# First stage of a bidirectional-WKV, attention and expert kernel: backward scan without the own key, minima read from PSUM and placed later, small vectors loaded first

## What is computed

```python
ek = exp(min(k, 30));  ekv = ek * v
nf[t] = nf[t-1] * decay + ekv[t];   df[t] = df[t-1] * decay + ek[t]      # forward in time
nb[t] = nb[t+1] * decay + ekv[t];   db[t] = db[t+1] * decay + ek[t]      # backward in time
euk = exp(min(u + k, 30))
num = nf + nb - ekv + euk * v
den = df + db - ek + euk
c = sigmoid(r) * (num / max(den, 1e-8)) * (0.8 + 0.2 * tf)
```

## Time and profile before

| what | value |
|---|---|
| median of three runs | 2295.05 us |
| the profiled execution's own time | 2294.41 us |
| its span | 2292.7 us |
| busy in the span: PE, DVE, ACT, POOL | 93%, 59%, 51%, 63% |
| end of the first stage (first instruction of the next) | 113.7 us |
| first query matmul, last one | 64.0 us, about 111 us |

### The profile page before, as it was taken

How to read it: one execution, slowest core, us unless ns; L and a number is a source line. 1 busy time by engine, 2 the same in 40 slices (tenths; PEclk the granted TensorE clock), 3 DMA queues, 4 the chain that set the end, 5 groups by cost and what they waited for, 6 DMA issues and landing times. The chain is left out here.

```text
span 2292.7 us, 39955 instructions
## 1 busy us (share of the span) xinstructions
PE 2143.2 (93%) x11247; PEld 1862.4 (81%) x11247; DVE 1349.4 (59%) x2499; ACT 1160.3 (51%) x2491; POOL 1439.5 (63%) x961
## 2 busy tenths in 40 slices
PE   2899999999999999999899989999999999999996
PEld 1678888888878878777777778989999999998874
DVE  8868888778856676766765433333333333333386
ACT  4477777787767767767652123333333333333310
POOL 7887777787755656666672311466677777653365
PEclk9999999999999999999998999999999999999998
DMA  5444444533365536665335543556667676664566
GB/s 129 140 124 133 129 134 161 169 118 100 121 232 163 161 116 211 216 197 185 115 128 202 203 143 118 159 168 185 192 189 210 185 210 187 200 194 134 171 199 205
DMA packets 367657, 380.29 MB, mean 166 GB/s; under 512 B 51556, under 2 KB 283560, under 8 KB 362728
## 3 DMA queue, kind: packets, MB, share of 16 engines
q1 hardware_dynamic: 255608, 252.20, 36.0%
q10 hardware_dynamic: 96496, 75.28, 10.6%
q0 software_dynamic: 15360, 50.34, 6.7%
HBM read 264.21 MB, written 120.59 MB: 168 GB/s over the span
## 5 line engine op out<-in xcount | busy, mean ns | idle before, releaser
L2066 POOL TENSOR_SCALAR we_high<-we_raw 128x1408 fp32r<-128x1408 f32 (+1 forms) x94 | 132.2, 1406 | 312.3 <-PE up_e L668 231.6
L2068 POOL TENSOR_TENSOR we_low<-we_raw,we_high 128x1408 fp32r<-128x1408 f32 (+1 forms) x94 | 312.2, 3321 | 7.8
L2281 DVE TENSOR_TENSOR hidden_e<-silu_e,up_e 128x352 f32<-128x352 f32 x127 | 66.2, 522 | 250.1 <-ACT silu_e L2220 248.3
L2264 DVE TENSOR_TENSOR hT_low<-hT_ps,hT_high 128x256 fp32r<-128x256 f32 x127 | 53.9, 425 | 253.1 <-ACT hT_high L2206 249.5
L2220 ACT ACTIVATE silu_e<-gate_e 128x352 f32<-128x352 f32 x127 | 59.1, 465 | 283.7 <-PE up_e L668 278.6
L668 PE MATMUL gate_e<-we_high,xT_high 128*128 x508 | 176.2, 347 | 11.5 <-DVE xT_low L2271 6.4
L2225 ACT ACTIVATE rows_out<-down_e 128x512 f32<-128x512 f32 x127 | 76.0, 599 | 198.6 <-PE down_e L668 194.2
L668 PE MATMUL gate_e<-we_high,xT_low 128*128 x508 | 164.5, 324 | 0.0
L668 PE MATMUL up_e<-we_high,xT_high 128*128 x508 | 164.3, 323 | 0.0
L668 PE MATMUL gate_e<-we_low,xT_high 128*128 x508 | 164.1, 323 | 0.0
L668 PE MATMUL up_e<-we_high,xT_low 128*128 x508 | 164.0, 323 | 0.0
(11 more groups left out here) (401 smaller groups left out, 7168.7 us busy)
## 6 DMA issues: line engine op xcount, KB each, us to landing
slots_out<-rows_out ACTq DMA_DIRECT2D x127, 256.0 KB
rows_early<-slots_in ACTq DMA_DIRECT2D x500, 64.0 KB
we_raw<-L_ffn_w_gate SPq DMA_DIRECT2D x32, 704.0 KB, 4.9
we_raw<-L_ffn_w_up SPq DMA_DIRECT2D x32, 704.0 KB, 5.2
w_ring<-L_attn_Wq SPq DMA_DIRECT2D x64, 256.0 KB
q_T<-q_out SPq DMA_DIRECT2D x64, 256.0 KB, 2.3
w_ring<-L_attn_Wk SPq DMA_DIRECT2D x64, 256.0 KB
w_ring<-L_attn_Wv SPq DMA_DIRECT2D x64, 256.0 KB
```

The lines of the kernel that those rows point to most:

```text
L2066: nc.gpsimd.tensor_scalar(wh[:, p, at:to], raw[:, at:to], 1.0, 1.0, ALU.mult, ALU.mult).then_inc(w_hi, 1)
L2068: nc.gpsimd.tensor_tensor(wl[:, p, at:to], raw[:, at:to], wh[:, p, at:to].bitcast(F32), ALU.subtract).then_inc(w_split, 1)
L2281: nc.vector.tensor_tensor(hb[:], sg[:], psu[:], ALU.mult).then_inc(h_done, 1)
```

## The change

1. The backward scans run over the keys from the second on and write 511 elements: b[t] = (b[t+1] + src[t+1]) * decay, the own key left out; the last element is set to zero once, at the start. So the difference dl = eu - ek falls away, and the sums take `eu` in its place. `eu` gets a ring of four tiles.
2. The two minima read the PSUM bank `psk` and no longer the copy `kt`; the next transposes into that bank wait for the minima too.
3. The orders of TensorE, ScalarE, VectorE and GpSimd change.
4. SyncE issues the eight small vectors first; the time embedding goes to ScalarE's queue, second after the first keys, and keys 2 and 3 from there to SyncE's queue. The time embedding and keys 1 have semaphores of their own.
5. ScalarE copies keys 0 (`t0`) before it waits for the small vectors.

```diff
+EU_RING = 4
 FIRST_PE = (
-    "k0 v0 k1 x0 k2 x1 k3 k4 x2 k5 k6 x3 x4 k7 x5 Q0 Q1 Q2 Q3 Q4 x6 Q5 Q6 Q7 Q8 Q9 Q10 x7 Q11 Q12 Q13 Q14 Q15 "
+    "k0 v0 k1 x0 k2 x1 k3 x2 k4 x3 k5 x4 Q0 k6 x5 Q1 Q2 k7 Q3 Q4 x6 Q5 Q6 Q7 Q8 Q9 Q10 x7 Q11 Q12 Q13 Q14 Q15 "
 FIRST_ACT = (
-    "t0 t1 E0 E1 h0 F0 t2 h1 E2 h2 h3 t3 c0 F1 h4 E3 t4 h5 c1 h6 F2 h7 F3 E4 F4 t5 h8 E5 c2 h9 c3 e0 t6 h10 e1 t7 "
+    "t0 t1 E0 E1 h0 F0 t2 h1 E2 h2 h3 t3 c0 F1 h4 E3 t4 h5 c1 h6 F2 h7 F3 h8 c2 t5 h9 F4 c3 E4 E5 h10 e0 t6 e1 t7 "
     "h11 E6 e2 F5 e3 e4 F6 e5 c4 E7 e6 e7 h12 e8 h13 e9 c5 h14 e10 e11 h15 F7 e12 c6 e13 e14 c7 e15 "
 FIRST_DVE = (
-    "m0 m1 s0 s1 m2 f0 m3 l0 s2 f1 m4 l1 s3 f2 m5 f3 l2 l3 s4 m6 s5 f4 m7 s6 f5 l4 s7 f6 l5 f7 l6 l7 "
+    "m0 m1 s0 s1 m2 f0 m3 l0 s2 f1 l1 s3 f2 l2 f3 l3 m4 m5 s4 s5 f4 m6 l4 s6 m7 f5 l5 s7 f6 l6 f7 l7 "
 FIRST_POOL = (
-    "o0 p0 o1 p1 a0 a1 o2 q0 p2 q1 q2 o3 q3 a2 p3 q4 q5 a3 o4 q6 p4 q7 q8 o5 q9 p5 q10 a4 q11 o6 a5 p6 o7 p7 q12 "
+    "o0 p0 o1 p1 a0 a1 o2 q0 p2 q1 q2 o3 q3 a2 p3 q4 q5 a3 q6 q7 q8 o4 p4 q9 o5 p5 q10 a4 q11 o6 a5 p6 o7 p7 q12 "
     "q13 a6 q14 a7 q15 "
...
-            sp.dma_start(te[:], cond.partition_broadcast(P)).then_inc(v_in, 16)
             for at, v, n in vec:
                 sp.dma_start(rows[at:at + n, :], v.rearrange("(r p) -> r p", p=P)).then_inc(v_in, 16)
+            for n in range(2, KC):
+                sp.dma_start(kin[:, n, :, :], column(fs, n)).then_inc(k_in[1], 16)
...
-            def other_products(n):
+            def other_product(n):
                 p = n % 2
-                tt(dl[:, p, :], eu[:, p, :], ek[:, p, :], ALU.subtract).then_inc(products_done, 1)
-                pool.wait_ge(products_done, 3 * n + 2)
-                tt(dk[:, p, :], dl[:, p, :], kt[:, p, :], ALU.mult).then_inc(products_done, 1)
+                tt(dk[:, p, :], eu[:, n % EU_RING, :], kt[:, p, :], ALU.mult).then_inc(products_done, 1)
...
                 if n >= 2:
                     pe.wait_ge(kt_done, n - 1)
+                    pe.wait_ge(min_done, n - 1)
...
-            for n in range(KC):
-                act.dma_start(kin[:, n, :, :], column(fs, n)).then_inc(k_in[1 if 0 < n < KC else 0], 16)
+            act.dma_start(kin[:, 0, :, :], column(fs, 0)).then_inc(k_in[0], 16)
+            act.dma_start(te[:], cond.partition_broadcast(P)).then_inc(te_in, 16)
+            act.dma_start(kin[:, 1, :, :], column(fs, 1)).then_inc(k1_in, 16)
...
                 if n >= 2:
-                    act.wait_ge(products_done, 3 * (n - 1))
+                    act.wait_ge(products_done, 2 * (n - 1))
                 nc.scalar.activation(kt[:, n % 2, :], psk[n % 2][:], ACT.Copy).then_inc(kt_done, 1)
...
+            order = list(FIRST_ACT)
+            turns(order[:1], t=keys)
             act.wait_ge(x_T, 1)
             nc.scalar.activation(cols[:], psv, ACT.Copy).then_inc(cols_done, 1)
...
             nc.vector.memset(one[:], 1.0)
-            dve.wait_ge(v_in, 16 * (len(vec) + 1))
+            for last_of in (nb, db):
+                nc.vector.memset(last_of[:, :, S - 1:S], 0.0)
+            dve.wait_ge(te_in, 16)
...
                 if n >= 2:
-                    dve.wait_ge(products_done, 3 * (n - 1))
+                    dve.wait_ge(products_done, 2 * n - 3)
                     dve.wait_ge(scan_done, n - 1)
-                nc.vector.tensor_scalar(ek[:, p, :], kt[:, p, :], 30.0, None, ALU.min)
-                nc.vector.tensor_scalar(eu[:, p, :], kt[:, p, :], cols[:, V_U1 + i:V_U1 + i + 1], 30.0, ALU.add,
+                nc.vector.tensor_scalar(ek[:, p, :], psk[p][:], 30.0, None, ALU.min)
+                if n >= EU_RING:
+                    dve.wait_ge(sums_done, 2 * (n - EU_RING + 1))
+                nc.vector.tensor_scalar(eu[:, n % EU_RING, :], psk[p][:], cols[:, V_U1 + i:V_U1 + i + 1], 30.0, ALU.add,
                                         ALU.min).then_inc(min_done, 1)
...
                 col = dec[:, n:n + 1].broadcast_to([P, S])
+                after = dec[:, n:n + 1].broadcast_to([P, S - 1])
                 for f, b, src in ((nf, nb, ekv), (df, db, ek)):
                     nc.vector.tensor_tensor_scan(f[:, p, :], col, src[:, p, :], 0.0, ALU.mult, ALU.add)
-                    last = nc.vector.tensor_tensor_scan(b[:, p, ::-1], col, src[:, p, ::-1], 0.0, ALU.mult, ALU.add)
+                    last = nc.vector.tensor_tensor_scan(b[:, p, 0:S - 1][:, ::-1], src[:, p, 1:S][:, ::-1], after, 0.0,
+                                                        ALU.add, ALU.mult)
```

More of the change, by code:

```diff
@@ L105, in first_gates @@
         small = sb("small", [P, 64])
-        kt, ek, eu, ekv, dl, dk = (two(f"g0_{n}") for n in ("kt", "ek", "eu", "ekv", "dl", "dk"))
+        kt, ek, ekv, dk = (two(f"g0_{n}") for n in ("kt", "ek", "ekv", "dk"))
+        eu = sb("g0_eu", [P, EU_RING, S])
         nf, nb, df, db = (two(f"g0_{n}") for n in ("nf", "nb", "df", "db"))
@@ L117, in first_gates @@
         psv, dec = vec_ps[:, 0:V_N], vec_ps[:, P:P + N]
-        v_in = sem("v_in")
+        v_in, te_in, k1_in = sem("v_in"), sem("time_in"), sem("k_in_second")
         k_in, x_in = [sem("k_in_first"), sem("k_in_rest")], [sem("x_in0"), sem("x_in1")]
@@ L212, in sums @@
                 pool.wait_ge(scan_done, n + 1)
-                tt(nb[:, p, :], nf[:, p, :], nb[:, p, :], ALU.add)
-                tt(db[:, p, :], df[:, p, :], db[:, p, :], ALU.add).then_inc(sums_done, 1)
+                tt(nf[:, p, :], nf[:, p, :], nb[:, p, :], ALU.add)
+                tt(df[:, p, :], df[:, p, :], db[:, p, :], ALU.add).then_inc(sums_done, 1)
                 pool.wait_ge(sums_done, 2 * n + 1)
[L216 to L220, removed]
+                pool.wait_ge(products_done, 2 * n + 2)
+                tt(nf[:, p, :], nf[:, p, :], dk[:, p, :], ALU.add)
+                tt(df[:, p, :], df[:, p, :], eu[:, n % EU_RING, :], ALU.add).then_inc(sums_done, 1)
+            turns(FIRST_POOL, o=first_product, p=other_product, q=low, a=sums)
         @block.tensor
@@ L226, in keys @@
             def keys(n):
-                pe.wait_ge(k_in[0 if n == 0 else 1], 16 if n == 0 else 16 * (KC - 1))
+                if n == 0:
+                    pe.wait_ge(k_in[0], 16)
+                elif n == 1:
+                    pe.wait_ge(k1_in, 16)
+                else:
+                    pe.wait_ge(k_in[1], 16 * (KC - 2))
                 if n >= KC:
@@ L252, in vectors @@
             def vectors(n):
-                pe.wait_ge(v_in, 16 * (len(vec) + 1))
+                pe.wait_ge(v_in, 16 * len(vec))
                 nc.tensor.transpose(psv, rows[:], ident[0:V_N, 0:V_N]).then_inc(x_T, 1)
@@ L276, in exponentials @@
                 nc.scalar.activation(ek[:, p, :], ek[:, p, :], ACT.Exp)
-                nc.scalar.activation(eu[:, p, :], eu[:, p, :], ACT.Exp).then_inc(exp_done, 1)
+                nc.scalar.activation(eu[:, n % EU_RING, :], eu[:, n % EU_RING, :], ACT.Exp).then_inc(exp_done, 1)
             def factor(n):
@@ L308, in _ @@
             nc.scalar.activation(small[:, 8:16], small[:, 0:8], ACT.Exp, scale=-1.0).then_inc(s_chain, 1)
-            order = list(FIRST_ACT)
-            turns(order[:1], t=keys)
             act.wait_ge(t_chain, 1)
@@ L338, in scans @@
                 p = n % 2
-                dve.wait_ge(products_done, 3 * n + 1)
+                dve.wait_ge(products_done, 2 * n + 1)
                 if n >= 2:
```

## The result

The changed kernel takes 2310.25 us (median of 11, 2304.8 to 2319.18) beside 2299.19 us of the kernel before (11 runs in all, 2294.31 to 2309.56): ratio 1.0047, 95% interval 1.0031 to 1.0063, so 7 to 14.5 us slower. The forecast was 13.6 us slower (2308.0). That 2308.0 and 2310.25 lie so close is in part luck: the forecast started from 2294.41, and the median of the kernel before over 11 runs is 2299.19.

What follows compares the result with a forecast made beforehand. VectorE's and GpSimd's recurrence was taken to bound the first stage until Q0, then TensorE's queries beside that recurrence. The gain to Q0, two stalls, slow restarts and smaller terms summed to +13.6 on 2294.41, giving 2308.0 us; range 2297 to 2316.

Steps and rivals of the forecast that it cites:

- Rival (c): TensorE after Q0: the queries stay unbroken if unit 6's exponentials are over by about 73 us, time 2290; chance 13%.
- (d): VectorE's swapped backward scan costs as attention's median one: +1.06 on sixteen scans, +17 us, 2325; chance 5%.
- (e): VectorE's minima: PSUM does not help them beside GpSimd, m stays at 2, +4 us, 2312; chance 4%.
- The slow restarts: TensorE after each of its two waits: Q4 and Q8 run slowly, 5.38 us against 2.72 warm; +2.7 us each.
- first pause: TensorE before Q4: it waits for the eviction of Q2 to empty a bank, from 73.5 to 81.0 us; +7.5.
- second pause: TensorE before Q8: it waits for the eviction of Q6, from 95.2 to 99.2 us; +4.0.
- gain to Q0: Start of the first query on TensorE: 57.9 us in place of 64.0; -6.1.
- k6, x5, k7 among the queries: TensorE after Q0: these three turns now run among the queries; +1.9 us or so.
- slow Q4: TensorE after its first wait: this query costs 5.4 us; +2.7.
- slow Q8: TensorE after its second wait: this query is slow again and ends at 104.5 us; +2.7.
- the tail: End of the first stage, from Q9's gated chunk through the last fractions; +0.9 us.
- Rival (b): The same stalls on TensorE but milder, without slow restarts or with two more gained at the start: +8, 2302.5; chance 10%.

Runs made afterwards that it cites:

- one order taken back: The changed kernel with m6, m7 and l4 to l7 back in their old places on VectorE; ratio to the kernel before 0.9967.
- old orders: The changed kernel's operations and early loads with all four orders of the kernel before; ratio to the kernel before 0.9955, in a second set of runs 0.9953.
- the evictions first: The changed kernel with ScalarE's order alone altered, evictions moved ahead of the exponentials of units 6 and 7; ratio to the kernel before 0.9991.

## Why the prediction was right

Right, by its own steps:
- The two stalls, their places, their releasers and about their sizes: 7.5 and 4.0 us forecast, 9.0 and 4.1 measured. Rival (c), unbroken queries, fell: Q3 ended at 69.5 and E6 began at 76.62. So did (d) (scan 1.19) and (e) (minima 0.68 and 0.74). PSUM made m 1.3 us, as taken from L334.
- The slow restarts. The granted clock is 0.50 from 74 us on, inside the first pause, and Q4, begun at 78.49, was evicted from 83.41: 4.9 us in place of 2.7. In the second pause the clock reads 1.00 (92 to 96) and then 0.55 (96 to 98); Q8 took 4.6 us.
- The cause was shown, not only argued: the orders alone reproduce both pauses, one order taken back removes both, and l4 to l6 taken back remove the second.

Off in size: the sum says 13.6, the stage end moved by 9.7. Its terms, with a query's length from its first matmul to the start of its eviction:

| term | forecast | measured |
|---|---|---|
| gain to Q0 | -6.1 | -8.6 |
| Q0 shorter than before (4.5 for 5.4) | not in the sum | -0.8 |
| k6, x5, k7 among the queries | +1.9 | +1.15 |
| first pause | +7.5 | +9.0 |
| slow Q4 | +2.7 | +2.2 |
| second pause | +4.0 | +4.1 |
| slow Q8 | +2.7 | +1.9 |
| what is left, the tail | +0.9 | +0.8 |

- The start was the largest miss. I took the first minima at 9.0 and the first scan at 13.2; they came at 7.0 and 11.1. The small vectors were there by 6.3, three us sooner than 9.3 before, and I had allowed for two at most, so that my bounds (8.5 to 9.95) did not hold the value. That is 2.1 of the 3.9 us.
- Slow queries. I took 5.38 from the one row of before; Q0 took 4.5 (55.41 to 59.95), Q4 4.9, Q8 4.6. On the path, Q4 and Q8, this is 1.2 us. One row was too little for a length that varies from run to run.
- The first pause is longer than forecast (9.0 for 7.5) though its end and Q0 both came 2.5 us sooner than I had them. From Q0 to the end of Q3 TensorE took 14.1 us and not 15.6, because Q0 was shorter and the transposes were too dear in my sum. Time saved ahead of a release that does not move with it only turns into pause.
- Rival (b), the same stalls but milder, at +8 us and 10%, held in part. One of its two conditions came (the start gained two us more), the other did not (both restarts were slow). The measured 9.7 lies nearer to its 8 than to my 13.6, so the forecast was right in mechanism and too high in size.
- That VectorE and GpSimd are both full before Q0 I had right; I did not say that each edit alone would be worth so little.

I wrote that within half a percent the runs would not be told from no change. Eleven runs did tell it: the interval is 0.31% to 0.63%. The chance for slower by over 0.5% was 0.54, for within 0.45; the measured 0.47% lies just inside the second, and the interval holds both. My sum of 13.6 us is 0.59%; with the start and the restarts sized as they came it would have been on the other side of the mark.

## What to carry over

In kernels with written-out orders, follow each moved turn to the in-order queues of its consumers: here minima moved two turns later on VectorE, the exponentials that need them stood in front of evictions on ScalarE, and the idle time appeared on TensorE. When two engines are both full, an edit that empties one is worth little until the other is emptied as well, so test such edits together and the reordering by itself. A change that bundles operations, loads and orders can hide a gain of 10 us under a loss of 20.

## What the hardware showed beside this

- An fp32 minimum over 128x512 from PSUM takes 0.67 to 0.74 us in all sixteen cases. From SBUF it takes 0.43 to 0.48 with GpSimd at rest; beside it the first of a pair took 0.40 to 1.59 and the second 1.48 to 1.51. Alone the PSUM form is slower by half; beside GpSimd the pair is faster.
- The length of TensorE's slow stretch at the first queries differs between runs of one kernel: with the old orders 4.0 and 5.1 us from Q0's first matmul to the start of its eviction. That alone moves the end of the stage by 1 us.
- The granted clock in a profile does not show every slow stretch. In the profile before it reads 1.00 from 64 to 68 us, while Q0's matmuls follow each other every 0.43 us, and every 0.23 us once warm. The step between matmuls is the surer sign.
- The length of a pause alone does not tell whether a slow stretch follows. With the evictions first, the pause of 2.35 us before 78.39 left the clock at 1.00 and the matmuls at full pace, and the one of 2.28 us before 106.57 was followed by a clock of 0.50 from 108 us on.
- A later stage with equal code took 83 us in one set of runs and 95 to 97 in the others, a difference larger than the whole effect studied here. With 83 us (old orders, first set) TensorE is busy throughout at a granted clock of 1.00; with 96.7 (old orders, second set) it is busy 88.2 us at 0.93 and pauses several times, once for 3.8 us. What starts these pauses is open.
